# Padding the products on 64 rows and on 64 or 32 columns to full 128 by 128

## The chip, the cores and the metric

The kernel runs on one core of a Trainium2 chip. The metric is the device time of one execution in microseconds (us), lower is better. Matrix products run on TensorE (PE in the profile, its weight loads apart as PEld), elementwise work on VectorE (DVE), ScalarE (ACT) and GpSimd (POOL). Transfers are issued by SyncE (SP).

## What is computed

The reference is one transformer-like layer on x of shape (4, 512, 128): a gated convolution block, then a mixture of 160 small experts, each behind a layer norm with a scale and a shift.

```python
h = _layernorm(x) * (1 + ca) + sa
# attention-free block: D = 128, DI = 256
h = _rmsnorm(h, norm_w); h = _linear(h, in_w, in_b)
gate, val = sigmoid(h[..., :DI]), h[..., DI:]
a = dwconv4(val) @ A @ Bm                 # then ha_w
b = linear(silu(dwconv9(val)), pw_w)      # then hb_w
x = x + ga * (h_in + linear(gate * fuse(concat(a, b)), out_w))
h = _layernorm(x) * (1 + cb) + sb
# experts: 160 of them, top 8, inner size 64
probs = sigmoid(h @ router_w.T + expert_bias)
combine = top-8 weights of probs, normalised, times 2.5
routed = sum_e (silu(h @ w_gate[e].T) * combine[:, e]) @ w_down[e]
shared = silu(h @ w_gate_shared.T) @ w_down_shared.T
x = x + gb * (routed + shared)
```

## The kernel before

The batch is worked in four chunks c = 0 to 3 of 512 tokens. Most products carry a value as the sum of two half-precision parts (a high and a low one). The helper `split` (lines 954 to 956) therefore issues three half-precision matmuls for one product, each on 512 columns of tokens: one at L954, one at L955, one at L956. Every such product in the kernel has these three lines, so they are told apart by the tiles they read.

The experts are taken in pairs, and two pairs make a duo. A chunk has 40 duos, the kernel 160. `duo(J)` issues on PE two up-projections of duo J (`bank<-x_h,w`, each 3 matmuls) and two down-projections of duo J-4 (`bank<-g_all,w`, each 3 matmuls). Between them ACT applies silu (L648), DVE multiplies by the routing weights (L931), ACT rounds to half precision (L667), and DVE takes the remainder (L927). The routing weights come from DRAM, where `c_out` has put them, and are loaded for every duo (L409).

`walk` is the order of the work, written out by hand, and every engine follows it. Chunk 0's block, and most of chunk 1's, run in a prologue before the first duo. After that, the steps of chunk c+1 (table `REST`) and c+2 (tables `FRONT` and `TAPS`) are put between the duos of chunk c, so the router of chunk 1 runs between the duos of chunk 0, and so on. The steps that matter here, on PE:

- `conv0`, `conv1`: nine taps of three matmuls each, then one matmul for the borders and the bias, on 64 rows: `rsym` (64 rows) against the constant `isym` (L1042). Twice a chunk, 8 in all.
- `logit`: for each of 4 groups of 128 tokens, one matmul on 64 rows for the expert bias (`ones2` against `rrtr`, L1109), and one `split` product of 160 columns (`bank<-rsg_h,x_h`). 16 groups in all. ACT's `prob` (L630) follows, then the top-8 search on DVE (L901, L905, L911, L921).
- `shup`: the shared expert's up-projection. Its stationary operand is the last 64 columns of `rsg_h` and `rsg_l`, so 64 rows of the result bank are written. One `split` product a chunk, followed by ACT's silu `ss` (L636).
- `cT`: the routing weights (160 columns) turned by transposes. Four turn columns 0 to 127 (L1122), four turn the other 32 columns (L1125). ACT copies the result to `cT0` and `cT1` (L641, L643), and SP writes it to DRAM (L426, L428).
- the shared expert's down-projection, `sdw` against `ss32`, both on 64 rows and in single precision (L1150). One a chunk, at the first down-projection of the chunk. It waits until ACT has emptied the accumulator of the chunk before (L676). A single-precision matmul shows as two records.

The first rows of `rsym` and `rrtr` (0 to 31) are written by ACT and rows 32 to 63 by DVE in `setup(5)` and `setup(8)`, once. `rsg` and `sdf` are loaded once, in the prologue, ahead of the expert weights, and turned into `rsg_h`, `rsg_l` (L549, L765) and `sdw` (L551).

Of the kernel before, what the change touches and what calls it, by code (L numbers as in the profile page):

```python
# [209 lines left out]
def build(nc, x, vecs, mats, wmod_d, outT_d, consts, rows, frow_d, symT, rsgT, sdT, idf_c, w_d, out):  # L210
# [3 lines left out]
    with ExitStack() as ctx:  # L214
# [16 lines left out]
        outT = sb("outT", [P, ML, D])  # L231
        rsg = sb("rsg", [P, E + INTER])
        sdf = sb("sdf", [INTER, P])
        sdw = sb("sdw", [INTER, P])
        win_h, win_l = sb("win_h", [P, DI], F16), sb("win_l", [P, DI], F16)
# [5 lines left out]
        zs = sb("zs", [P, 2, L], F16)  # L241
        rsg_h, rsg_l = sb("rsg_h", [P, E + INTER], F16), sb("rsg_l", [P, E + INTER], F16)
        row4 = sb("row4", [B, MODC])
# [3 lines left out]
        ebias, outb = brow[0:64, 0:E], brow[:, E:E + D]  # L247
        rsym = sb("rsym", [64, DI], F16)
        rrtr = sb("rrtr", [64, E], F16)
        gob = sb("gob", [P, D])  # L250
# [15 lines left out]
        x_l = [sb(f"x_l{i}", [P, L], F16) for i in range(2)]  # L266
        ss32 = sb("ss32", [INTER, L])
        pr, key, cw = (sb(n, [P, NT, E]) for n in ("pr", "key", "cw"))
# [7 lines left out]
        yT = sb("yT", [P, L])  # L276
        cT0, cT1 = sb("cT0", [P, L]), sb("cT1", [E - P, L])
        dum = sb("dum", [P, 1])
# [30 lines left out]
        def k(name, rows=P):  # L309
# [3 lines left out]
        s = {n: sem(n) for n in (  # L313
            "ld_vec ld_wmod ld_mat ld_outT ld_cst ld_rows ld_frow ld_sym ld_rsg ld_sd ld_idf ld_mod row_out w_hi w_lo "
            "x_in0 x_in1 x_in2 x_in3 pool_zero pads zs_zero zs_one eps_set one_set scb_set mod_ps mod_half mod_set row_ps row_half row_set "
# [46 lines left out]
        def _(sp):  # L362
# [49 lines left out]
            def att(c, n):  # L412
                if n == "zmv":
                    if c:
                        sp.wait_ge(s["y_ps"], 2 * c)
                    else:
                        sp.wait_ge(s["zs_zero"], 1)
                        sp.wait_ge(s["zs_one"], 1)
                    sp.wait_ge(s["zh_set"], c + 1)
                    sp.wait_ge(s["zl_set"], c + 1)  # L420
                    for q in range(DC):
                        w = slice(32 * q, 32 * q + DS)
                        sp.dma_start(zs[w], zp[w, :, q:q + L]).then_inc(s["z_mv"], 16)
                elif n == "c_out":
                    sp.wait_ge(s["cT_set"], 2 * c + 1)
                    sp.dma_start(cd[c, 0:P, :], cT0[:]).then_inc(s["c_out"], 16)  # L426
                    sp.wait_ge(s["cT_set"], 2 * c + 2)
                    sp.dma_start(cd[c, P:E, :], cT1[:]).then_inc(s["c_out"], 16)  # L428

# [15 lines left out]
        def _(pool):  # L445
            g = nc.gpsimd
            g.memset(hnT[:, :, 0:PADL], 0.0).then_inc(s["pads"], 1)
            g.memset(hnT[:, :, PADL + L:], 0.0).then_inc(s["pads"], 1)
            g.memset(mhalf[:], -0.5).then_inc(s["eps_set"], 1)
            g.memset(eps5[:], 1e-5).then_inc(s["eps_set"], 1)  # L450
# [45 lines left out]
        def _(act):  # L496
# [13 lines left out]
            def setup(n):  # L510
# [18 lines left out]
                elif n == 5:  # L529
                    taps_hi(2)  # L530
                    act.wait_ge(s["sc_ps"], 1)
                    a(rsym[0:32], A3[0:32, 0:DI], ACT.Copy, scale=ES)
                    a(tmp_h[32:64, 0], A3[32:64, 0:DI], ACT.Copy, scale=ES).then_inc(s["sc_hi"], 1)
# [26 lines left out]
            def att(c, n):  # L560
# [71 lines left out]
                elif n == "ss":  # L632
                    act.wait_ge(s["sh_ps"], c + 1)
                    if c:
                        act.wait_ge(s["sd_ps"], c)
                    a(ss32[:], TB[0:INTER, :], ACT.Silu, scale=1.0 / ES).then_inc(s["ss_set"], 1)  # L636
                elif n == "cT_sb":
                    if c:
                        act.wait_ge(s["c_out"], 32 * c)
                    act.wait_ge(s["cT_ps"], 2 * c + 1)  # L640
                    a(cT0[:], A4[:], ACT.Copy).then_inc(s["cT_set"], 1)  # L641
                    act.wait_ge(s["cT_ps"], 2 * c + 2)
                    a(cT1[:], A3[0:E - P, :], ACT.Copy).then_inc(s["cT_set"], 1)  # L643

# [302 lines left out]
        def _(pe):  # L947
# [67 lines left out]
            def att(c, n):  # L1015
# [15 lines left out]
                elif n[0:4] == "conv":  # L1031
# [7 lines left out]
                    if i1 == KS:  # L1039
                        if c + q == 0:  # L1040
                            pe.wait_ge(s["sc_lo"], 1)
                        mm(bk[:], rsym[:, q * P:(q + 1) * P], k("isym", 64), start=False, stop=True).then_inc(s["conv_ps"], 1)  # L1042
                elif n == "z":
# [53 lines left out]
                elif n == "logit":  # L1097
# [6 lines left out]
                    for t in range(NT):  # L1104
# [3 lines left out]
                        dst = (A4, A3)[t // 2][:, t % 2 * E:(t % 2 + 1) * E]  # L1108
                        mm(dst, k("ones2", 64), rrtr[:], start=True, stop=False)  # L1109
                        b = c % 2  # L1110
# [3 lines left out]
                elif n == "shup":  # L1114
                    pe.wait_ge(s["xl_set"], c + 1)
                    b = c % 2
                    split(TB[0:INTER, :], (rsg_h[:, E:], rsg_l[:, E:]), (x_h[b][:], x_l[b][:])).then_inc(s["sh_ps"], 1)
                elif n == "cT":
# [5 lines left out]
                    for t in range(NT):  # L1124
                        last = turn(A3[0:E - P, t * P:(t + 1) * P], cw[:, t, P:E], idf[:])  # L1125
                    last.then_inc(s["cT_ps"], 1)
# [102 lines left out]
```

## Time and profile before

| | |
|---|---|
| median of 3 runs | 573.82 us (571.63 to 575.61) |
| the profiled execution's own time | 573.52 us |
| its span, first to last instruction | 571.7 us |
| mean granted TensorE clock | 0.987 |
| busy in the span: PE, DVE, ACT, POOL | 544.1, 474.0, 414.4, 29.6 us |

A matmul's duration in a record includes the time that it takes to run through the array, while the next one has already begun. The duration of a record is therefore not what it costs. The cost is read from the distance between the starts of one matmul and the next. In a timeline, the first column is the start in us, the second the duration in us, and `x4` means that four like instructions were merged into one row. A note in brackets at the end is the time that the engine sat idle before it, with what ended the wait.

### The profile page before, as it was taken

To read this page: it belongs to the slowest core of one execution; us is meant where nothing else is said; L and a number is where in the kernel's file an instruction comes from. 1 tells how busy PE (TensorE), PEld (TensorE's weight loads), DVE (VectorE), ACT (ScalarE), POOL (GpSimd) and SP (SyncE) were. 2 spreads that over 40 slices of the span, in tenths; PEclk is the share of its full clock that TensorE was granted. 3 is DMA by queue.
4 is the path that set the end of the run, shared out by engine and by line. 5 is a ranking of instruction groups with operands and counts; after the bars stand their busy time and mean duration, and the time that the engine had idled before them with its cause. 6 is when DMAs were issued, how large, how long until landed. Compare 5 with 4: busy or idle time off the path is not lost.

```text
span 571.7 us, 7315 instructions
## 1 busy us (share of the span) xinstructions
PE 544.1 (95%) x2528; PEld 251.4 (44%) x2528; DVE 474.0 (83%) x600; ACT 414.4 (72%) x668; POOL 29.6 (5%) x52
## 2 busy tenths in 40 slices
PE   5697889999999999999999999999989999999996
PEld 3334424543444444454444444454434444444442
DVE  5676479999959988799859688789959988999995
ACT  5446488789777776779666686568876877777773
POOL 5011000050000000011000000002000000000000
PEclk9797999999999999999999999999999999999999
DMA  7976075445534655455544455455635666566650
GB/s 265 346 258 263 10 248 180 150 150 179 185 110 148 204 187 176 146 169 199 158 138 148 170 185 174 148 181 188 213 119 180 231 201 203 198 207 205 200 186 18
DMA packets 33244, 103.26 MB, mean 181 GB/s; under 512 B 3700, under 2 KB 9013, under 8 KB 32952
## 3 DMA queue, kind: packets, MB, share of 16 engines
q1 hardware_dynamic: 33208, 102.81, 53.3%
q8 instruction: 20, 0.33, 0.2%
q14 instruction: 16, 0.13, 0.1%
HBM read 99.90 MB, written 2.37 MB: 179 GB/s over the span
## 4 chain that ended last, share of the span: by engine, by line
PE 78%; DVE 9%; ACT 5%; issue 4%; DMA 2%; POOL 1%; SPq 0%; ACTq 0%; DVEq 0%
PE bank L954 24%; PE bank L955 24%; PE bank L956 24%; DVE g_all L927 2%; DVE s_all L931 2%; PE bank L1075 2%; ACT g_all L667 1%; DMA c_all<-combine 1%; PE bank L1085 1%; DMA g_all<-wmod_dram 1%; ACT s_all L648 1%; DVE w L791 1%; PE bank L1150 1%; ACT hnT L594 1%; PE bank L1109 0%
## 5 line engine op out<-in xcount | busy, mean ns | idle before, releaser
L648 ACT ACTIVATE s_all<-bank 128x512 f32<-128x512 f32 x320 | 189.4, 593 | 109.6 <-PE bank L956 105.9
L927 DVE TENSOR_TENSOR g_all<-s_all,g_all 128x1024 f16<-128x1024 f32 x160 | 195.3, 1221 | 55.6 <-ACT g_all L667 55.1
L931 DVE TENSOR_TENSOR s_all<-s_all,c_all 128x1024 f32<-128x1024 f32 x160 | 194.8, 1218 | 3.9 <-DMA c_all<-combine 3.4
L667 ACT ACTIVATE g_all<-s_all 128x1024 f16<-128x1024 f32 x160 | 168.0, 1050 | 3.4 <-DVE s_all L931 3.3
L954 PE MATMUL bank<-x_h,w 128*128 128x512 f16 x320 | 121.4, 380 | 4.1 <-ACT s_all L648 4.0
L954 PE MATMUL bank<-g_all,w 128*128 128x512 f16 x320 | 121.4, 379 | 2.7 <-DVE g_all L927 2.7
L955 PE MATMUL bank<-g_all,w 128*128 128x512 f16 x320 | 121.3, 379 | 0.0
L956 PE MATMUL bank<-g_all,w 128*128 128x512 f16 x320 | 121.3, 379 | 0.0
L956 PE MATMUL bank<-x_l,w 128*128 128x512 f16 x320 | 121.3, 379 | 0.0
L955 PE MATMUL bank<-x_h,w 128*128 128x512 f16 x320 | 121.3, 379 | 0.0
L954 PEld LDWEIGHTS bank<-x_h,w 128*128 128x128 f16 x320 | 31.3, 98 | 46.9 <-ACT s_all L648 10.0
L954 PEld LDWEIGHTS bank<-g_all,w 128*128 128x128 f16 x320 | 31.3, 98 | 44.7 <-DVE g_all L927 7.5
L956 PEld LDWEIGHTS bank<-g_all,w 128*128 128x128 f16 x320 | 31.3, 98 | 37.8
L956 PEld LDWEIGHTS bank<-x_l,w 128*128 128x128 f16 x320 | 31.3, 98 | 37.8
L955 PEld LDWEIGHTS bank<-g_all,w 128*128 128x128 f16 x320 | 31.3, 98 | 36.6
L955 PEld LDWEIGHTS bank<-x_h,w 128*128 128x128 f16 x320 | 31.3, 98 | 35.4 <-issue 2.0
L954 PE MATMUL bank<-hnT,wc_h 128*128 128x512 f16 x72 | 28.6, 397 | 1.2 <-ACT hnT L594 1.2
L955 PE MATMUL bank<-hnT,wc_l 128*128 128x512 f16 x72 | 28.5, 395 | 0.0
L956 PE MATMUL bank<-hnT,wc_h 128*128 128x512 f16 x72 | 28.3, 393 | 0.0
L791 DVE SCALAR_TENSOR_TENSOR w<-w 128x1024 f16<-128x1024 f32 x20 | 24.2, 1216 | 4.0 <-ACT w L558 3.9
L558 ACT ACTIVATE w<-w 128x1024 f16<-128x1024 f32 x20 | 20.8, 1052 | 5.0 <-DVE w L791 5.0
L484 POOL TENSOR_TENSOR mse<-ms,eps 128x4 f32<-128x4 f32 x4 | 6.0, 1496 | 193.2 <-ACT hr_h L575 193.2
(212 smaller groups left out, 367.6 us busy)
## 6 DMA issues: line engine op xcount, KB each, us to landing
c_all<-combine SPq DMA_DIRECT2D x160, 512.0 KB, 3.9
w<-w_dram SPq DMA_DIRECT2D x20, 512.0 KB, 8.9
s_all<-mats_dram SPq DMA_DIRECT2D x1, 1152.0 KB, 7.6
attw<-symT_dram SPq DMA_DIRECT2D x1, 1152.0 KB, 10.3
res<-x_dram SPq DMA_DIRECT2D x4, 256.0 KB, 9.0
combine<-cT SPq DMA_DIRECT2D x4, 256.0 KB, 3.1
out_dram<-res SPq DMA_DIRECT2D x4, 256.0 KB, 2.4
mod<-rows_mod SPq DMA_DIRECT2D x1, 960.0 KB, 6.5
```

Of the source, the lines that this page charges most:

```text
L484: g.tensor_tensor(mse[:], ms[:], eps6[:], ALU.add).then_inc(s["mse_set"], 1)
L558: a(high(i), staged(i), ACT.Copy, scale=ES).then_inc(s["w_hi"], 1)
L594: a(hnT[:, :, PADL:PADL + L], TBh.rearrange("p (a l) -> p a l", a=2), ACT.Copy)\
L648: a(sr[J % SRING][:, q * L:(q + 1) * L], U[q][:], ACT.Silu, scale=1.0 / ES).then_inc(s["s_done"], 1)
L667: a(gh[n % GRING], sr[n % SRING], ACT.Copy).then_inc(s["hi_set"], 1)
L791: e.scalar_tensor_tensor(out=low(i), in0=staged(i), scalar=ES, in1=high(i), op0=ALU.mult, op1=ALU.subtract).then_inc(s["w_lo"], 1)
L927: e.tensor_tensor(gl[n % GRING], sr[n % SRING], gh[n % GRING], ALU.subtract).then_inc(s["lo_set"], 1)
L931: e.tensor_tensor(sr[J % SRING], sr[J % SRING], cr[J % CRING], ALU.mult).then_inc(s["gm"], 1)
L954: mm(dst, lh, rh, start=start, stop=False)
L955: mm(dst, ll, rh, start=False, stop=False)
L956: return mm(dst, lh, rl, start=False, stop=stop)
L1075: last = mm((A1, A2)[q][:], wb[:, i, q * P:(q + 1) * P], s32[:, i, :], start=False, stop=(i == ML - 1))
```

## The change

The operands that had 64 rows get 128, the added ones zero. The operands that had 64 or 32 columns get 128.

- `rsym` and `rrtr` get 128 rows, and POOL sets them to zero at the start (two memsets). ACT waits for these (`rows_zero`) before it writes the first part of `rsym`. L1042 and L1109 read all 128 rows of the constants, whose added rows are zero already.
- `rsg` gets 64 zero columns behind its 224, and with it `rsg_h` and `rsg_l`. `shup` takes 128 columns and writes the whole bank, `ss32` has 128 rows.
- `sdf` and `sdw` get 64 zero rows, so the product at L1150 is on 128 rows.
- The second half of `cT` turns columns 32 to 159 in place of 128 to 159. The 32 wanted rows then are rows 96 to 127 of the bank, and the copy and the DRAM write take them from there.

```diff
-        rsg = sb("rsg", [P, E + INTER])
-        sdf = sb("sdf", [INTER, P])
-        sdw = sb("sdw", [INTER, P])
+        rsg = sb("rsg", [P, E + P])
+        sdf = sb("sdf", [P, P])
+        sdw = sb("sdw", [P, P])
...
-        rsg_h, rsg_l = sb("rsg_h", [P, E + INTER], F16), sb("rsg_l", [P, E + INTER], F16)
+        rsg_h, rsg_l = sb("rsg_h", [P, E + P], F16), sb("rsg_l", [P, E + P], F16)
...
-        rsym = sb("rsym", [64, DI], F16)
-        rrtr = sb("rrtr", [64, E], F16)
+        rsym = sb("rsym", [P, DI], F16)
+        rrtr = sb("rrtr", [P, E], F16)
...
-        ss32 = sb("ss32", [INTER, L])
+        ss32 = sb("ss32", [P, L])
...
-        cT0, cT1 = sb("cT0", [P, L]), sb("cT1", [E - P, L])
+        cT0, cT1 = sb("cT0", [P, L]), sb("cT1", [P, L])
...
-                    sp.dma_start(cd[c, P:E, :], cT1[:]).then_inc(s["c_out"], 16)
+                    sp.dma_start(cd[c, P:E, :], cT1[2 * P - E:]).then_inc(s["c_out"], 16)
...
+            g.memset(rsym[:], 0.0).then_inc(s["rows_zero"], 1)
+            g.memset(rrtr[:], 0.0).then_inc(s["rows_zero"], 1)
...
+                    act.wait_ge(s["rows_zero"], 2)
...
-                    a(ss32[:], TB[0:INTER, :], ACT.Silu, scale=1.0 / ES).then_inc(s["ss_set"], 1)
+                    a(ss32[:], TB[:], ACT.Silu, scale=1.0 / ES).then_inc(s["ss_set"], 1)
...
-                    a(cT1[:], A3[0:E - P, :], ACT.Copy).then_inc(s["cT_set"], 1)
+                    a(cT1[2 * P - E:], A3[2 * P - E:, :], ACT.Copy).then_inc(s["cT_set"], 1)
...
-                        mm(bk[:], rsym[:, q * P:(q + 1) * P], k("isym", 64), start=False, stop=True).then_inc(s["conv_ps"], 1)
+                        mm(bk[:], rsym[:, q * P:(q + 1) * P], k("isym"), start=False, stop=True).then_inc(s["conv_ps"], 1)
...
-                        mm(dst, k("ones2", 64), rrtr[:], start=True, stop=False)
+                        mm(dst, k("ones2"), rrtr[:], start=True, stop=False)
...
-                    split(TB[0:INTER, :], (rsg_h[:, E:], rsg_l[:, E:]), (x_h[b][:], x_l[b][:])).then_inc(s["sh_ps"], 1)
+                    split(TB[:], (rsg_h[:, E:], rsg_l[:, E:]), (x_h[b][:], x_l[b][:])).then_inc(s["sh_ps"], 1)
...
-                        last = turn(A3[0:E - P, t * P:(t + 1) * P], cw[:, t, P:E], idf[:])
+                        last = turn(A3[:, t * P:(t + 1) * P], cw[:, t, E - P:], idf[:])
```

The host adds the zero columns to `rsg` and the zero rows to `sdT`. All else is as before.

## Rows read from the trace of the kernel before

**Rows 1.** The page's part 1: busy time, share and instructions of each engine.

```profile
PE 544.1 (95%) x2528; PEld 251.4 (44%) x2528; DVE 474.0 (83%) x600; ACT 414.4 (72%) x668; POOL 29.6 (5%) x52
```

**Rows 2.** Windows: stretch, length, busy PE, PEld, DVE, ACT, POOL, clock, DMA.

```profile
20.00:40.00 20.00, 20.00 (x80) 9.17 (x78) 12.69 (x46) 6.02 (x12) 2.48 (x2) 0.89 0.71 270
139.00:414.00 275.00, 274.64 (x1297) 127.57 (x1296) 234.89 (x270) 203.68 (x318) 7.64 (x6) 1.00 0.51 169
```

**Rows 3.** Timeline of PE: start, duration, line, tiles, shapes; the end of a convolution.

```profile
166.51 0.38 PE L954 MATMUL bank<-hnT,wc_h 128*128 128x512 f16 x1
...
166.94 0.38 PE L956 MATMUL bank<-hnT,wc_h 128*128 128x512 f16 x1
167.26 0.39 PE L1042 MATMUL bank<-cst,rsym 64*128 64x512 f16 x1
167.57 0.39 PE L954 MATMUL bank<-hnT,wc_h 128*128 128x512 f16 x1
167.80 0.38 PE L955 MATMUL bank<-hnT,wc_l 128*128 128x512 f16 x1
```

**Rows 4.** Timeline of PE: router and shared up-projection of chunk 1.

```profile
157.00 0.38 PE L956 MATMUL bank<-g_all,w 128*128 128x512 f16 x1
...
157.49 0.24 PE L954 MATMUL bank<-rsg_h,x_h 128*128 128x160 f16 x1
157.56 0.23 PE L955 MATMUL bank<-rsg_h,x_l 128*128 128x160 f16 x1
157.63 0.23 PE L956 MATMUL bank<-rsg_l,x_h 128*128 128x160 f16 x1
...
159.09 0.23 PE L956 MATMUL bank<-rsg_l,x_h 128*128 128x160 f16 x1
159.26 0.40 PE L954 MATMUL bank<-x_h,rsg_h 128*64 128x512 f16 x1
...
160.02 0.39 PE L954 MATMUL bank<-x_h,w 128*128 128x512 f16 x1
```

**Rows 5.** Timeline of PE: the transposes of the routing weights, chunk 1.

```profile
187.02 0.60 PE L1122 MATMUL bank<-idf,cw 128*128 128x128 f32 x4
187.45 0.60 PE L1125 MATMUL bank<-idf,cw 128*32 128x128 f32 x4
187.89 0.38 PE L954 MATMUL bank<-hnT,wc_h 128*128 128x512 f16 x1
```

**Rows 6.** Groups by line and form: weight loads of these transposes; busy us, mean ns.

```profile
L1122 PEld LDWEIGHTS bank<-idf,cw 128*128 128x128 f32 x16 | 1.8, 141 | 3.2 <-DVE cw L921 2.9
...
L1125 PEld LDWEIGHTS bank<-idf,cw 128*32 128x32 f32 x16 | 1.6, 97 | 0.1
```

**Rows 7.** Timeline of PE: the shared down-projection of chunk 1.

```profile
215.21 1.12 PE L1150 MATMUL bank<-ss,sdw 64*128 64x512 f32 x2 [0.18 <-ACT yT L676]
216.26 0.39 PE L954 MATMUL bank<-g_all,w 128*128 128x512 f16 x1
```

**Rows 8.** Timeline of PE: single-precision products on 128 rows, in the prologue's wake.

```profile
95.19 1.88 PE L1075 MATMUL bank<-attw,wb 128*128 128x512 f32 x4
96.91 0.38 PE L954 MATMUL bank<-x_h,w 128*128 128x512 f16 x1
```

**Rows 9.** Chain of waits in order of time, prologue: start, us, what.

```profile
22.24 0.43 PE bank L954
...
65.12 0.45 ACT pr L630
```

**Rows 10.** Timeline of DVE in the prologue.

```profile
45.64 0.39 DVE L765 SCALAR_TENSOR_TENSOR rsg_l<-rsg,rsg_h 128x224 f16<-128x224 f32 x1
```

**Rows 11.** Timeline of ACT behind the router of chunk 3.

```profile
418.60 0.60 ACT L648 ACTIVATE s_all<-bank 128x512 f32<-128x512 f32 x1 [3.38 <-PE bank L956]
```

**Rows 12.** Timeline of ACT behind the router of chunk 1.

```profile
168.74 0.59 ACT L648 ACTIVATE s_all<-bank 128x512 f32<-128x512 f32 x1
```

**Rows 13.** Timeline of PE, the up-projection that waits for the silu of rows 12.

```profile
169.53 0.38 PE L954 MATMUL bank<-x_h,w 128*128 128x512 f16 x1
```

More of the change, by code:

```diff
@@ L313, in build @@
         s = {n: sem(n) for n in (
-            "ld_vec ld_wmod ld_mat ld_outT ld_cst ld_rows ld_frow ld_sym ld_rsg ld_sd ld_idf ld_mod row_out w_hi w_lo "
+            "rows_zero ld_vec ld_wmod ld_mat ld_outT ld_cst ld_rows ld_frow ld_sym ld_rsg ld_sd ld_idf ld_mod row_out w_hi w_lo "
             "x_in0 x_in1 x_in2 x_in3 pool_zero pads zs_zero zs_one eps_set one_set scb_set mod_ps mod_half mod_set row_ps row_half row_set "
@@ L1196 @@
         w["in_w"].T, w["in_w"][DI:], w["ha_w"].T, w["hb_w"].T, w["pw_w"], w["fuse_w"].T)], 1)
-    rsg = np.concatenate([f["router_w"].T, f["w_gate_shared"].T], 1)
+    spare = np.zeros((P, P - INTER), np.float32)
+    rsg = np.concatenate([f["router_w"].T, f["w_gate_shared"].T, spare], 1)
     two = np.zeros((P, P), np.float32)
@@ L1217 @@
               "consts": consts.astype(np.float16), "rows": rows, "frow": w["fuse_b"][None],
-              "symT": w["sym_k"].reshape(DI, KS).T.reshape(1, KS * DI), "rsgT": rsg, "sdT": f["w_down_shared"].T,
+              "symT": w["sym_k"].reshape(DI, KS).T.reshape(1, KS * DI), "rsgT": rsg, "sdT": np.concatenate([f["w_down_shared"].T, spare.T]),
               "idf": np.eye(P, dtype=np.float32), "w": wall}
```

## Prediction

> **What bounds the kernel now.** I began with the busy times. PE is busy for 95% of the span [rows 1], DVE for 83%, so PE is the first suspect. The table of stretches says where this holds: from 139 to 414 us PE is busy 274.64 of 275 us, at the full granted clock of 1.00, that is 2.4 GHz, while DVE is busy 234.89 [rows 2]. "Busy" hides short stalls, since a record lasts 0.38 us and the next starts sooner, so I then went through the PE timeline by starts. In the normal stream three matmuls of 512 columns lie within 0.43 us from first start to last, 0.216 a step (166.51 to 166.94 is two steps) [rows 3]. Wherever a start comes later than that, PE has lost time that no busy figure shows. In this stretch nearly all such losses sit beside matmuls on 64 rows or with 64 columns.
>
> The prologue, a stretch before 139 us and one behind the router of chunk 3 are bounded by chains through ACT, DVE and DMA. There I followed the chain of waits in order of time, to see which changed products lie on it.
>
> **The border product of a convolution (L1042, 8 of them).** From the last full matmul at 166.94 to the second one behind it at 167.80 there are 0.86 us for three steps [rows 3]. Three normal steps are 0.65. The 64-row product starts 0.32 after its predecessor, its successor 0.31 after it, and one more step is 0.01 late: 0.21 us lost around a matmul that itself streams the same 512 columns. With 128 rows I take all of it to go. Four of the eight (chunks 2 and 3) lie between duos of the PE-bound stretch: 4 x 0.21 = 0.84 us. One of chunk 1's lies on the prologue's chain (below). Both of chunk 0's and the second of chunk 1's lie where PE afterwards waits for DVE, ACT or a DMA. That wait covers them, and I count nothing (0.6 us if the cover were gone).
>
> The Trainium skill, page TensorEngine Tiling (Array Packing), section Tiling Modes, Key Properties, says that a change of tiling mode drains TensorE. That would make 64 rows, and 64 columns, modes of their own, entered and left each time, which is what the starts show; it gives no duration, and the sum needs none from it.
>
> **Router and shared up-projection (L1109, `rsg_h`).** A full product of 160 columns takes 0.07 us from start to start (157.56 to 157.63) [rows 4]. By columns alone it would be 0.216 x 160/512 = 0.068, so I take 0.069. From 157.00 to the first up-projection at 160.02 there are 3.02 us. In full shape this is 0.216 + 16 x 0.069 + 3 x 0.216 = 1.97. With the 0.01 behind it, 1.06 us are saved a chunk. Part of this is the 64-column product: its first matmul starts 0.17 after its predecessor, not 0.07, and from its start to the next duo there are 0.76 us where 3 x 0.216 = 0.65 would do; its share is 0.22, that of the 64 rows 0.84.
>
> Chunks 1 to 3 save this on the path: 3 x 1.06 = 3.18 us. For chunk 3 the time behind it is bounded by ACT and DVE, not PE. But ACT was idle for 3.38 us waiting just for this up-projection [rows 11], so it starts 1.06 earlier, and the chain behind it shifts whole.
>
> **Prologue.** The chain runs through PE, including one border product, up to the end of the router of chunk 0, then to `prob` at 65.12 [rows 9], the top-8 search, the transposes and the DRAM round trip of the routing weights. The saving is 0.21 + 0.84 = 1.05 us; `shup` is off this chain.
>
> **The shared down-projection (L1150, 4).** Its two records and the step to the next take 1.05 us [rows 7]. Single-precision products on 128 rows take (96.91 - 95.19) / 4 = 0.43 each [rows 8], so 0.86 for two: 0.20 saved with the 0.01 behind. The wait in front of it, for ACT's L676, stays. Chunk 0's is covered by a wait for DVE. 3 x 0.20 = 0.60 us.
>
> **The transposes (L1125, 16).** Wide ones take 187.45 - 187.02 = 0.43 for four, narrow ones 0.44 [rows 5]. Nothing is lost at the 32 columns, so nothing is won. The load of 128 columns lasts 141 ns against 97 [rows 6], but lies beside the products, since the wide ones already keep the pace. Without that cover: 16 x 44 ns = 0.7 us.
>
> Here a rule speaks against the change. The Trainium skill, TensorE: Matmul & The Clock Gate, section LDWEIGHTS, puts a load at its column count over 1.2 GHz, so four times as long for 128 as for 32. By it the 16 loads would grow by 80 ns each, an estimate of 1.3 us if exposed; the trace grows them by 44 ns and hides them.
>
> **Additions.** The two POOL memsets come before POOL's first wait, for the statistics of chunk 0, which come later than they end. ACT comes to its new wait only behind the first convolution weights, and so long after them that nothing queues behind it. `rsg_l` works on 288 columns in place of 224: 0.39 us [rows 10] becomes at most 0.39 x 288/224 = 0.50, 0.11 more on DVE, ahead of the gating of chunk 0. This is beside the chain, which runs through chunk 1's normalisation then; 0.1 us if not. The loads of `rsg` and `sdf` grow by 64 KB together, ahead of the weights on SP's queue; at the 270 GB/s of that time [rows 2] this is 0.24 us on weights that are used later. The silu, copies and DRAM write keep their columns; partitions are free. For these together: 0 to 0.4, taken 0.
>
> **Sum.** 1.05 + 3.18 + 0.84 + 0.60 = 5.67 us. The profiled execution took 573.52, so 567.85; the median of the runs is 0.30 higher, so 568.15, rounded to **568.2 us**, 1.0% below.
>
> **Rivals.**
>
> A. *Part of the gain turns into waits.* Where PE speeds up, the slack to ACT and DVE must hold. The tightest place I found behind a router is the up-projection at 169.53, whose silu ended at 168.74 + 0.59 = 169.33 [rows 12, 13]: 0.20 us, while the border product at 167.26 gives 0.21. That costs 0.01. Larger losses would need the prologue's or chunk 3's chain to hold on something that doesn't move, say the DMA of the routing weights. Without these two, 1.05 + 1.06 less: 5.67 - 2.11 = 3.56 saved, **570.3 us**. Against it: the 3.38 us of idle ACT. Chance 0.08.
>
> B. *Only the rows cost, not the columns.* Then the three `shup` on the path keep 0.22 each: 5.0 saved, **568.8 us**. Or the wide weight loads show, 0.7: the same figure. Against it: starts are late on entering and on leaving the 64 columns [rows 4]. But the transposes show that 32 columns need not cost [rows 5]. Chance 0.07.
>
> C. *The change doesn't do what it says:* the late starts come from something else about these products (a constant as an operand, the start of an accumulation). **573.8 us**. Against it: three kinds with nothing else in common show the same 0.1 on each side. Chance 0.04.
>
> D. *Slower:* the granted clock. At half clock (1.2 GHz) a matmul of 512 columns takes 0.43 us, as at 22.24 [rows 9], where the stretch's clock is 0.89 [rows 2]. The router of chunk 0 gets shorter, while the waits around it (the search, then the DRAM round trip) stay, so PE is idle for a larger share of 60 to 83 us. If the clock fell there and stayed low into the first duos, each matmul would cost 0.21 more. It decides from 5.67 / 0.21 = 27 matmuls on, some 12 us at half clock. For over 1% slower it takes twice that, **579.6 us**. Against it: PE already waits there, and with 0.89 in one early stretch [rows 2] the mean over the whole span is still 0.987, which leaves little at half clock later. Chance 0.03.
>
> The forecast itself has 0.78.
>
> **How the numbers follow.** About 1% is what a measurement of this kernel can tell from no change. That bound lies at 568.08, within 0.1 us of the forecast, so the forecast's chance is split between faster and the same. Three runs of before spread over 4 us, which puts 1.5 us on either side of a median. More mechanisms take from the sum than add to it. Faster by over 1%: 0.45, from the forecast (0.43) and B (0.02). Within 1%: 0.52, the rest of the forecast (0.35), the rest of B (0.05), A and C. Slower: 0.03, which is D. The range goes up to A with some spread on it, 571.3, and down by the spread and for a chain that gives more than its sum, 565.8. C, D and the tails are left out.
>
> **What would show it.** Right: starts 0.216 apart through each border product; router and `shup` of chunks 1 to 3 in 1.97 us; two records of L1150 in 0.86; the same 0.11 for each transpose; the idle ACT at 418 down from 3.38 to 2.3. Wrong: starts still late by 0.1 at these products (C, or B where only `shup` is late), new idle time in front of L954 with ACT or DVE as the releaser (A), a clock under 1.00 between 60 and 100 us (D).

## The result and the profile after

| | before | after |
|---|---|---|
| median of 4 runs of each, side by side | 574.14 us (571.63 to 575.61) | 566.68 us (565.39 to 569.14) |
| the profiled execution's own time | 573.52 us | 567.25 us |
| its span | 571.7 us | 565.2 us |
| mean granted TensorE clock | 0.987 | 0.986 |

The ratio is 0.9897, with the interval [0.9873, 0.9921]. (The quotient of the two medians is 0.9870; four runs of each leave a difference of that size, and I use the ratio with its interval.) Two later series of the same kernel gave 0.9929 [0.9913, 0.9945] and 0.9908 [0.9892, 0.9924]; in the first of them one execution took 2006 us and is left out. The mean of the three is 0.991, against 568.15 / 573.82 = 0.990 forecast. Whether the gain is over or under 1%, which the forecast left open, these intervals leave open too. Lines stand three lower than before: L954 to L956 are now L957 to L959, L1042 is L1045, L1150 is L1153.

Part 1 of the page of the kernel after, which answers to [rows 1]:

```profile
PE 537.8 (95%) x2528; PEld 253.4 (45%) x2528; DVE 474.6 (84%) x600; ACT 415.4 (73%) x668; POOL 29.4 (5%) x54
```

PE has as many instructions as before and 6.3 us less busy time, and the span is 6.5 us shorter.

The PE timeline of the kernel after, the end of a convolution, which answers to [rows 3]:

```profile
163.59 0.38 PE L959 MATMUL bank<-hnT,wc_h 128*128 128x512 f16 x1
163.81 0.38 PE L1045 MATMUL bank<-cst,rsym 128*128 128x512 f16 x1
164.02 0.38 PE L957 MATMUL bank<-hnT,wc_h 128*128 128x512 f16 x1
```

The starts are 0.22 and 0.21 apart. The 0.1 on each side is gone. Next, the router and the shared up-projection of chunk 1, which answer to [rows 4]:

```profile
154.71 0.38 PE L959 MATMUL bank<-g_all,w 128*128 128x512 f16 x1
154.93 0.23 PE L1112 MATMUL bank<-rrtr,cst 128*128 128x160 f16 x1
...
155.97 0.23 PE L959 MATMUL bank<-rsg_l,x_h 128*128 128x160 f16 x1
156.03 0.38 PE L957 MATMUL bank<-x_h,rsg_h 128*128 128x512 f16 x1
...
156.68 0.38 PE L957 MATMUL bank<-x_h,w 128*128 128x512 f16 x1
```

From 154.71 to 156.68 there are 1.97 us, as forecast, in place of 3.02.

I then set the starts of the same matmul in both traces against each other, all through the program. The lead of the kernel after, in us:

| up to | lead | what gave it |
|---|---|---|
| 52.4 us, second convolution of chunk 0's block | 0.02 | |
| end of the router of chunk 0 | 2.55 | 1.45 from a shorter stretch at half clock, 1.08 from the change |
| first down-projection of a duo, 80.59 | 2.28 | 0.27 lost again |
| router and `shup` of chunk 1 | 3.34 | 1.06 |
| border products of chunk 2 | 3.68 | -0.06 in front of an up-projection, 0.40 |
| behind `sdw` of chunk 1 | 3.78 | 0.10 |
| router and `shup` of chunk 2 | 4.85 | 1.07 |
| border products of chunk 3, `sdw` of chunk 2 | 5.37 | 0.41, 0.11 |
| router and `shup` of chunk 3, its `sdw` | 6.52 | 1.06, 0.09 |

The 1.45 us are no work of the change: in the profile of before, a stretch at half clock (starts 0.43 us apart) lasts from 48.5 to 55.3 us, in that of after only from 47.8 to 51.2. The windows show it, in the column in front of the last two; before, then after:

```profile
40.00:60.00 20.00, 16.06 (x67) 8.27 (x65) 11.64 (x28) 13.11 (x33) 2.42 (x4) 0.83 0.63 252
```

```profile
40.00:60.00 20.00, 16.05 (x74) 9.22 (x75) 11.39 (x28) 13.32 (x34) 2.42 (x4) 0.91 0.61 243
```

The length of this stretch doesn't go with the change. In the runs below it is 6.8 us again in `x64cols` and `late`, which have all of the change, and 3.4 us in `grouped`, which pads nothing. So the change itself gave 6.52 - 1.45 = 5.07 us, where 5.67 were forecast.

### The profile page after: what moved, and what is told of

Read it like the earlier page. It is cut to its first block, busy times and chain, and to the rows that moved or that the text cites. A ratio compares the mean times of both kernels' runs of the same rounds, so it can differ in the third digit from the quotient of the medians.

```text
span 565.2 us, 7318 instructions
## 1 busy us (share of the span) xinstructions
PE 537.8 (95%) x2528; PEld 253.4 (45%) x2528; DVE 474.6 (84%) x600; ACT 415.4 (73%) x668; POOL 29.4 (5%) x54
## 4 chain that ended last, share of the span: by engine, by line
PE 78%; DVE 9%; ACT 6%; issue 4%; DMA 2%; POOL 0%; SPq 0%; ACTq 0%; DVEq 0%
PE bank L957 24%; PE bank L959 24%; PE bank L958 24%; DVE g_all L930 2%; DMA attw<-symT_dram 2%; PE bank L1078 2%; DVE s_all L934 2%; ACT g_all L670 1%; ACT s_all L651 1%; PE bank L1088 1%; PE bank L1153 1%; DVE w L794 1%; ACT hnT L597 1%; ACT w L561 0%; ACT yT L679 0%
## 5 line engine op out<-in xcount | busy, mean ns | idle before, releaser
L930 DVE TENSOR_TENSOR g_all<-s_all,g_all 128x1024 f16<-128x1024 f32 x160 | 195.4, 1221 | 52.4 <-ACT g_all L670 51.9
L957 PE MATMUL bank<-x_h,w 128*128 128x512 f16 x320 | 121.4, 379 | 3.9 <-ACT s_all L651 3.7
L957 PE MATMUL bank<-g_all,w 128*128 128x512 f16 x320 | 121.3, 379 | 2.1 <-DVE g_all L930 2.1
L959 PE MATMUL bank<-g_all,w 128*128 128x512 f16 x320 | 121.3, 379 | 0.0
L959 PE MATMUL bank<-x_l,w 128*128 128x512 f16 x320 | 121.3, 379 | 0.0
L957 PEld LDWEIGHTS bank<-x_h,w 128*128 128x128 f16 x320 | 31.3, 98 | 46.0 <-ACT s_all L651 10.0
L957 PEld LDWEIGHTS bank<-g_all,w 128*128 128x128 f16 x320 | 31.3, 98 | 42.0 <-DVE g_all L930 5.0
L959 PEld LDWEIGHTS bank<-g_all,w 128*128 128x128 f16 x320 | 31.3, 98 | 37.8
L959 PEld LDWEIGHTS bank<-x_l,w 128*128 128x128 f16 x320 | 31.3, 98 | 37.8
L957 PE MATMUL bank<-hnT,wc_h 128*128 128x512 f16 x72 | 28.5, 396 | 1.2 <-ACT hnT L597 1.2
L959 PE MATMUL bank<-hnT,wc_h 128*128 128x512 f16 x72 | 28.8, 400 | 0.0
```

The lines of the kernel that those rows point to most:

```text
L930: e.tensor_tensor(gl[n % GRING], sr[n % SRING], gh[n % GRING], ALU.subtract).then_inc(s["lo_set"], 1)
L957: mm(dst, lh, rh, start=start, stop=False)
L959: return mm(dst, lh, rl, start=False, stop=stop)
```

## What the theory and its rivals are now

The theory: TensorE is late by about 0.1 us on entering a product on 64 rows or with 64 columns, and by as much again on leaving it. The rivals: only rows cost (B); something else about these products costs (C). Three things were open after the result: where the limit lies, whether the cost goes by product or by change of shape, and why the prologue gave back 0.27 us (rival D, at a small scale).

## Experiment 1: the disputed cost by itself

A product is added to each of the 160 duos of the kernel after, in the middle of an up-projection. It multiplies zeros, so nothing in the result changes. `x128` is the control with a full product, `x64rows` has 64 rows, `x64cols` 64 columns.

```diff
+        zt = sb("zt", [P, P], F16)          # zeros
...
-                        split(U[q][:], pair(J, q, 0), (x_h[b][:], x_l[b][:])).then_inc(s["up_ps"], 1)
+                        (wh, wl), xh = pair(J, q, 0), x_h[b]
+                        mm(U[q][:], wh, xh[:], start=True, stop=False)
+                        mm(U[q][:], wl, xh[:], start=False, stop=False)
+                        if q == 0:
+                            mm(U[q][:], zt[:], xh[:], start=False, stop=False)              # x128
+                            mm(U[q][:], zt[0:64], xh[0:64], start=False, stop=False)        # x64rows
+                            mm(U[q][0:64], zt[:, 0:64], xh[:], start=False, stop=False)     # x64cols
+                        mm(U[q][:], wh, x_l[b][:], start=False, stop=True).then_inc(s["up_ps"], 1)
```

Only one of the three marked lines stands in each kernel.

> The changed kernel with one more half-precision matmul in each of the 160 duos: a tile of zeros as the stationary operand, on 128 rows and 128 columns, 512 columns of tokens, between the second and the third matmul of the duo's first up-projection. It adds zero to the result. It is the control for the two runs beside it. All theories: 160 x 0.216 = 34.6 us, less a little where DVE and ACT bound the time. With 567 us for the changed kernel, about 600 us. Starts 0.216 apart around the added matmul.

> As the control, but the added matmul is on 64 rows (zeros and the first 64 rows of the tokens), between matmuls on 128 rows. Theory (a change of the number of rows costs 0.10 us on entering and 0.10 on leaving): 0.21 us more for each of the 160, so 33 us above the control, about 632 us, with the added matmul 0.31 behind its predecessor and its successor 0.31 behind it. Rival C (the late starts came from other properties of the three products, such as a constant as operand or the start of an accumulation; none of these is here): the same as the control, 600 us.

> As the control, but the added matmul has 64 stationary columns and writes 64 rows of the bank. Theory (a change of columns costs like a change of rows): about 0.2 us each, 632 us. Rival B (only rows cost, the columns in shup were late for another reason): 600 us, as the control.

| | median, us | ratio to before |
|---|---|---|
| x128 | 597.06 | 1.0441 [1.0403, 1.0479] |
| x64rows | 627.69 | 1.0970 [1.0938, 1.1003] |
| x64cols | 631.08 | 1.1011 [1.0966, 1.1056] |

Against the control, 64 rows cost 30.6 us more, 0.19 for each of 160, and 64 columns 34.0 us, 0.21 each. The PE timelines of one place show it; first the control, then 64 rows, then 64 columns. The added product is at L1152.

```profile
301.37 0.38 PE L1150 MATMUL bank<-x_h,w 128*128 128x512 f16 x1
301.59 0.38 PE L1152 MATMUL bank<-x_h,zt 128*128 128x512 f16 x1
301.81 0.38 PE L1153 MATMUL bank<-x_l,w 128*128 128x512 f16 x1
```

```profile
301.54 0.38 PE L1150 MATMUL bank<-x_h,w 128*128 128x512 f16 x1
301.85 0.39 PE L1152 MATMUL bank<-x_h,zt 64*128 64x512 f16 x1
302.17 0.39 PE L1153 MATMUL bank<-x_l,w 128*128 128x512 f16 x1
```

```profile
300.78 0.38 PE L1150 MATMUL bank<-x_h,w 128*128 128x512 f16 x1
301.09 0.40 PE L1152 MATMUL bank<-x_h,zt 128*64 128x512 f16 x1
301.42 0.39 PE L1153 MATMUL bank<-x_l,w 128*128 128x512 f16 x1
```

In the control all steps are 0.22. With 64 rows or columns the step to the product is 0.31, the step from it 0.32 or 0.33, and the one behind it 0.22 or 0.23. Operand, accumulation and place are the same in all three, so C is out for good, and so is B: columns cost as much as rows. The control adds some 30 us over the kernel after, not 160 x 0.216 = 34.6. Before 139 us PE is not always the bound: in the window from 102 to 139 us it was busy 35.08 of 37 us before and 36.98 in the control, so part of the added work went into idle time.

## Experiment 2: where the limit lies

`shapes` is the kernel after with other counts of rows and columns at the places that the change touches. The places with 32 rows leave out the low part of the bias.

```diff
+                        r = {(1, 0): 33, (2, 0): 32, (2, 1): 96, (3, 0): 64, (3, 1): 65}.get((c, q), P)
+                        mm(bk[:], rsym[0:r, q * P:(q + 1) * P], k("isym", r), start=False, stop=True).then_inc(s["conv_ps"], 1)
...
+                        r = {1: (32, 64, 96, 33), 2: (48, 65, 80, 112), 3: (64, 32, 64, 128)}.get(c, (P,) * NT)[t]
+                        mm(dst, k("ones2", r), rrtr[0:r], start=True, stop=False)
...
+                    n_ = {1: 96, 2: 80, 3: 65}.get(c, P)
+                    split(TB[0:n_], (rsg_h[:, E:E + n_], rsg_l[:, E:E + n_]), (x_h[b][:], x_l[b][:])).then_inc(s["sh_ps"], 1)
```

> The changed kernel with other numbers of rows at single places, to read the starts there. Border products: 33 rows (chunk 1, first), 32 and 96 rows (chunk 2), 64 and 65 rows (chunk 3). Bias products of the router: 32, 64, 96, 33 rows in chunk 1, 48, 65, 80, 112 rows in chunk 2, 64, 32, 64, 128 in chunk 3. Shared up-projection on 96, 80 and 65 columns in chunks 1 to 3. The places with 32 rows leave out the low part of the border or bias. Theory (the array is set to a tile of 32, 64 or 128 rows, and what lies between is rounded up): 32, 33, 48 and 64 rows show 0.10 on each side, 65, 80, 96 and 112 rows show nothing, and so for the columns, where 96, 80 and 65 show nothing. Rival (anything short of 128 costs): all show 0.10 on each side. The time moves by 1 to 2 us against the changed kernel.

Its one execution took 569.14 us, which says nothing by itself. Its PE timeline does. Router of chunk 1, with 32 rows, then 96, then 33:

```profile
154.81 0.38 PE L959 MATMUL bank<-g_all,w 128*128 128x512 f16 x1
155.12 0.24 PE L1114 MATMUL bank<-rrtr,cst 32*128 32x160 f16 x1
155.29 0.24 PE L957 MATMUL bank<-rsg_h,x_h 128*128 128x160 f16 x1
...
155.92 0.23 PE L959 MATMUL bank<-rsg_l,x_h 128*128 128x160 f16 x1
155.99 0.23 PE L1114 MATMUL bank<-rrtr,cst 96*128 96x160 f16 x1
156.07 0.23 PE L957 MATMUL bank<-rsg_h,x_h 128*128 128x160 f16 x1
...
156.21 0.23 PE L959 MATMUL bank<-rsg_l,x_h 128*128 128x160 f16 x1
156.37 0.24 PE L1114 MATMUL bank<-rrtr,cst 33*128 33x160 f16 x1
```

The steps to and from 32 rows are 0.31 and 0.17, those to and from 96 rows 0.07 and 0.08, and that to 33 rows is 0.16. The other places agree. 32, 33, 48 and 64 rows are late by 0.1 on each side; 65, 80, 96 and 112 rows not at all. For columns, 65 (the up-projection at chunk 3) is enough too:

```profile
412.45 0.23 PE L959 MATMUL bank<-rsg_l,x_h 128*128 128x160 f16 x1
412.52 0.38 PE L957 MATMUL bank<-x_h,rsg_h 128*65 128x512 f16 x1
...
413.17 0.38 PE L957 MATMUL bank<-x_h,w 128*128 128x512 f16 x1
```

The Trainium skill, TensorEngine Tiling (Array Packing), section Tiling Modes, lists 32, 64 and 128 rows and columns as the configurations, and says that changing between them drains the engine. By that rule 65 rows, which no tile of 64 holds, would run as 128. The trace agrees: a padding of one row beyond 64 is enough, and all 128 aren't needed.

## Experiment 3: by product or by change of shape

`grouped` is the kernel before, with only the order in the router changed: the four 64-row bias products first, then the four `split` products. With this goes that the wait for `x2_set` comes ahead of the first of them, and that of the two groups of a bank only the first has `start=True`.

```diff
+                    dst = [(A4, A3)[t // 2][:, t % 2 * E:(t % 2 + 1) * E] for t in range(NT)]
+                    pe.wait_ge(s["x2_set"], c + 1)
                     for t in range(NT):
-                        if t == 2:
-                            pe.wait_ge(s["x2_set"], c + 1)
+                        mm(dst[t], k("ones2", 64), rrtr[:], start=(t % 2 == 0), stop=False)
+                    for t in range(NT):
...
-                        dst = (A4, A3)[t // 2][:, t % 2 * E:(t % 2 + 1) * E]
-                        mm(dst, k("ones2", 64), rrtr[:], start=True, stop=False)
...
-                        last = split(dst, (x_h[b][:, w], x_l[b][:, w]), (rsg_h[:, 0:E], rsg_l[:, 0:E]), start=False)
+                        last = split(dst[t], (x_h[b][:, w], x_l[b][:, w]), (rsg_h[:, 0:E], rsg_l[:, 0:E]), start=False, stop=bool(t % 2))
```

> The kernel before, nothing padded, but the four bias products on 64 rows of a chunk's router stand together, ahead of the four split products, so that the number of rows changes once in and once out in place of four times. Theory (the cost sits at a change of rows, not at a product on 64 rows): two of the four starts stay late, 0.21 us, and 3 x 0.21 = 0.63 us go in each chunk, 2.5 us in all, ratio 0.9956. The four 64-row products start 0.07 apart. Rival (each product on 64 rows costs, wherever it stands): they start 0.16 or more apart, and the time stays at 574.

It took 569.62 us, a ratio of 0.9967 [0.9948, 0.9986]. Its PE timeline, chunk 1:

```profile
158.06 0.38 PE L956 MATMUL bank<-g_all,w 128*128 128x512 f16 x1
158.38 0.45 PE L1107 MATMUL bank<-rrtr,cst 64*128 64x160 f16 x4
158.76 0.24 PE L954 MATMUL bank<-rsg_h,x_h 128*128 128x160 f16 x1
```

The step into the group is 0.32. From the first of the four to the matmul behind them there are 0.38: three steps of about 0.07 and a last one of 0.16. So four 64-row products in a row pay once, and it is the change of shape that costs, not the product. Of 0.84 a router this order saves some 0.63, or 2.5 us for four, 0.44%, forecast as 0.9956. The ratio agrees, but its interval alone would also allow 0.14%; the steps carry this.

## Experiment 4: one part alone, and the kernels once more

`rows_only` is the kernel before with the padding of rows in `rsym`, `rrtr` and the constants alone. `shup`, `sdw` and the transposes keep their shapes. The two memsets and the wait for `rows_zero` are in it too. `again` and `again2` are the kernel after and `before_again` the kernel before, unchanged.

```diff
-        rsym = sb("rsym", [64, DI], F16)
-        rrtr = sb("rrtr", [64, E], F16)
+        rsym = sb("rsym", [P, DI], F16)
+        rrtr = sb("rrtr", [P, E], F16)
...
-                        mm(bk[:], rsym[:, q * P:(q + 1) * P], k("isym", 64), start=False, stop=True).then_inc(s["conv_ps"], 1)
+                        mm(bk[:], rsym[:, q * P:(q + 1) * P], k("isym"), start=False, stop=True).then_inc(s["conv_ps"], 1)
...
-                        mm(dst, k("ones2", 64), rrtr[:], start=True, stop=False)
+                        mm(dst, k("ones2"), rrtr[:], start=True, stop=False)
```

> The kernel before with only the rows of the half-precision products padded (the border product and the router's bias, L1042 and L1109); the shared expert's two products and the transposes stay narrow. Theory: of the sum, the prologue's 1.05, three routers at 0.84 and four border products at 0.21 remain: 4.4 us saved, ratio 0.992. The shared up-projection still starts 0.17 behind its predecessor and the next duo 0.31 behind it.

> The changed kernel once more, for its ratio and for where the half clock (1.2 GHz) lies in another execution. Theory (the profiled execution owed about 1.4 us of its 6.5 to a half-clock stretch that ended sooner, which is luck): over more executions the ratio comes nearer to 1 - 5.2/574 = 0.991. Rival (the change itself brings the clock up sooner): the half-clock stretch at 48 to 55 us is short here too, and the ratio is 0.988 or less.

> The kernel before, profiled once more. Theory (where the half clock ends is luck): its half-clock stretch near 50 us ends at another time than 55.3 us, or has another length than 6.8 us. Rival (the kernel sets it): the same place and length as before, within 0.3 us.

> The changed kernel once more on another occasion. Theory (the sum holds but for 0.3 us at the shared down-projection and 0.3 us in the DMA round trip of the prologue, and the clock adds or takes some 1.5 us from one execution to the next): ratio 0.990 to 0.992. Rival (the shorter router costs clock on average): 0.993 or more, and mean granted clocks lower than in the runs of the kernel before beside it.

`rows_only` took 566.69 us, ratio 0.9912 [0.9878, 0.9947]; `before_again` 572.64 us in its one execution; `again` and `again2` gave the ratios told above.

On where the half clock lies, `again` says nothing, since its profile is of the execution of 2006 us. In `again2` the stretch near 50 us is 3.4 us long, from 48.0 to 51.4, nearly as in the kernel after. In `before_again` there is none near 50 us, as the theory of luck allowed. The rival that expected a ratio of 0.993 or more with lower mean clocks is right about the clocks: 0.987 on average in `again` and `again2`, against 0.990 in the runs of the kernel before beside them. The ratios are 0.9929 and 0.9908, one at its border and one not. I come back to this below.

By the steps, `rows_only` should lack 3 x (0.22 + 0.10) = 0.96 us, or 0.17%, of the change. The intervals are wider than that, so the times don't separate the two. The PE timeline does; here the shared up-projection of chunk 1 in `rows_only`:

```profile
155.36 0.23 PE L959 MATMUL bank<-rsg_l,x_h 128*128 128x160 f16 x1
155.52 0.40 PE L957 MATMUL bank<-x_h,rsg_h 128*64 128x512 f16 x1
...
156.29 0.39 PE L957 MATMUL bank<-x_h,w 128*128 128x512 f16 x1
```

It starts 0.16 after its predecessor, not 0.06 as in the kernel after, and 0.77 us pass to the next duo, not 0.65.

## What the prologue gave back

The prologue was forecast to give 1.05 us. It gave 1.08 by the end of the router, but 0.27 were lost before the first down-projection. The windows of 20 us from 60 to 80 show the place (stretch, length, busy PE, PEld, DVE, ACT, POOL, clock, DMA share, GB/s): before, then a second profile of it, then `rows_only`, then the kernel after.

```profile
60.00:80.00 20.00, 16.67 (x85) 7.04 (x84) 9.32 (x22) 12.90 (x20) 0.00 (x0) 1.00 0.32 107
```

```profile
60.00:80.00 20.00, 16.36 (x84) 6.92 (x83) 10.17 (x23) 13.34 (x21) 0.00 (x0) 1.00 0.38 123
```

```profile
60.00:80.00 20.00, 16.01 (x83) 6.88 (x80) 12.42 (x25) 14.15 (x23) 0.00 (x0) 1.00 0.42 154
```

```profile
60.00:80.00 20.00, 16.69 (x81) 7.57 (x80) 12.58 (x25) 13.99 (x22) 0.00 (x0) 0.91 0.41 155
```

The clock falls to half for a time in the kernel after, and not in the others. The chain of waits of the kernel after (start, us, what) names who feels it:

```profile
71.31 0.43 PE bank L959
71.74 0.27 PE bank L1045
72.08 0.60 ACT attw L604
...
79.90 0.86 PE bank L1153 x2
```

These are taps of the second convolution of chunk 1, at 0.43 a step from 68.3 to 71.7 us. Before, the chain ran here through the DRAM round trip of the routing weights instead:

```profile
71.38 1.79 DMA combine<-cT
...
73.88 5.35 DMA c_all<-combine
```

The time from the first transpose of `cT` to the first down-projection of a duo, in the profiles that have the same order of work between the two:

| kernel | half clock between 60 and 90 us | PE idle before `cT`, us | cT to down-projection, us |
|---|---|---|---|
| before | none | 1.70 | 82.88 - 69.59 = 13.29 |
| before_again | none | 1.70 | 82.02 - 68.84 = 13.18 |
| rows_only | none | 1.69 | 79.99 - 66.93 = 13.06 |
| after | 68.3 to 71.7 | 1.92 | 80.59 - 67.05 = 13.54 |
| again2 | 68.5 to 71.9 | 1.92 | 81.21 - 67.67 = 13.54 |
| shapes | 66.9 to 70.3 | 1.92 | 80.68 - 66.71 = 13.97 |
| grouped | 78.7 to 85.5 | 1.83 | 82.43 - 67.55 = 14.88 |

With the stretch, the kernel after takes 0.25 us more than before and 0.48 more than `rows_only`. In `shapes` it falls on the transposes themselves and takes 0.68 more than before. In `grouped`, which pads nothing, it falls on the first duos and takes 1.6 more.

A stretch near 70 us stands in all seven profiles that have the full change and none of the fillers of experiment 5 (after, again2, shapes, late and the three of experiment 1), in neither of before and not in `rows_only`. That is the place and the mechanism of rival D, at a small part of the loss that would have made the kernel slower. Of the shapes that `rows_only` keeps, the shared down-projection can't bring the stretch on, since it comes at 79.7 us. The shared up-projection can: padded, it is over 0.22 us sooner, and PE then waits 1.92 us in front of the transposes in place of 1.70. That fits D, but no run changes it alone, and `grouped` shows that such a stretch can come without the change. With one profile for most kernels this is an association, not a proof.

The mean clocks of the other executions point the same way. They average 0.987 in each of `again`, `again2` and `late`, against 0.990 in the runs of the kernel before beside them and 0.9915 in `rows_only`. One stretch of 3.4 us at half clock takes 3.4 x 0.5 / 566 = 0.003 from the mean, an estimate. But it isn't in every execution: two of the first four had 0.986 and 0.987, the other two 0.994, and these two were the fastest, 565.39 and 566.12 us.

## Experiment 5: no half clock, and no wait at the shared down-projection

`warm` is the kernel after with 34 useless matmuls in places where PE would be idle in the prologue. They write to a bank that nobody reads before it is started anew. In the order of the cuts they stand before the first transposes of chunk 0, behind these of chunks 0 and 1, before the output projection of chunk 0, and before the transposes of its routing weights.

```diff
+            def spin(k_):
+
+                for _ in range(k_):
+                    mm(U1[:], k("id"), k("isym"))
...
+                    if c == 0:
+                        pe.wait_ge(s["mod_half"], 2)
+                        spin(11)
...
+                    if c < 2:
+                        spin(4)
...
+                        if c == 0:
+                            spin(7)
...
+                    if c == 0:
+                        spin(8)
```

`late` is the kernel after with both up-projections of a chunk's first duo ahead of its first down-projection, so that the wait for ACT's L679 is over when PE comes to it. `best` has both.

```diff
-                for q in range(2):
+                def up(q):
...
+                def down(q):
...
+                if d == 0:
+                    up(0), up(1), down(0), down(1)
+                else:
+                    up(0), down(0), up(1), down(1)
```

> The changed kernel with idle PE time in the prologue filled by matmuls whose result is not used (identity against the constant of the border product, into a free bank): 11 before the first transposes of chunk 0, 4 behind these of chunks 0 and 1, 7 before chunk 0's output product, 8 before chunk 0's routing weights are turned. Theory (the half clock comes from PE's waits in the prologue, and what it costs is what spreads the times): the half-clock stretches near 17 to 24 us and 48 to 51 us shrink or go, their matmuls start 0.216 and not 0.43 apart, the mean granted clock rises above 0.995, and the time falls by 2 to 5 us against the changed kernel, with less spread. Rival (the half clock comes at these times whatever PE does): the same time or up to 2 us more, for the added matmuls that run over into work.

> The changed kernel with another order at the first duo of a chunk: both up-projections ahead of the shared down-projection and the two down-projections, so that the wait of PE for ACT's emptying of the accumulator is covered. Theory: the start of L1153's product behind its predecessor falls from 0.56 to 0.22 us and its first record's step from 0.53 to 0.43, 0.44 us at three places: 1.3 us. Rival (ACT and DVE wait in its stead): the next down-projections start late and nothing is won.

> Both additions together: the filled prologue and the later wait. If both theories hold, 3 to 6 us below the changed kernel.

| | median, us | ratio to before |
|---|---|---|
| again2 | 567.09 (566.80 to 567.71) | 0.9908 [0.9892, 0.9924] |
| warm | 563.49 (562.87 to 566.15) | 0.9853 [0.9833, 0.9874] |
| late | 567.19 (565.34 to 568.72) | 0.9901 [0.9884, 0.9918] |
| best | 563.09 (561.66 to 565.94) | 0.9843 [0.9820, 0.9866] |

`warm` is 3.6 us faster than the kernel after. The smaller spread that was expected did not come: its executions lie 3.3 us apart, all at mean clocks of 0.997 to 1.000, so the spread has another source besides. Its windows have the full clock throughout the prologue:

```profile
0.00:20.00 20.00, 12.68 (x63) 7.36 (x64) 13.17 (x39) 12.57 (x35) 10.26 (x38) 1.00 0.92 301
20.00:40.00 20.00, 18.70 (x84) 9.12 (x83) 14.28 (x47) 8.51 (x16) 2.48 (x2) 1.00 0.83 311
40.00:60.00 20.00, 18.93 (x107) 10.18 (x106) 11.32 (x31) 12.28 (x32) 2.41 (x4) 1.00 0.53 208
60.00:80.00 20.00, 17.59 (x81) 7.40 (x79) 14.14 (x24) 15.87 (x23) 0.00 (x0) 1.00 0.57 187
```

Its last router product of chunk 0 starts at 58.92, against 62.30 in the kernel after; from there the time from `cT` to the down-projection is 76.47 - 63.67 = 12.80, against 13.54. Together that is 4.1 us, the difference of the spans (561.1 and 565.2). The Trainium skill, TensorE: Matmul & The Clock Gate, section HAM oscillation, says that a kernel with waits between its bursts of matmuls swings between the two clocks, and advises to restructure it. The traces agree that idle stretches and half clock go together: in the first 20 us PE is busy 9.86 us at a mean clock of 0.93 in the kernel after, and 12.68 us at 1.00 in `warm`; in front of the transposes of `cT` it is idle for 1.92 us and for 0.20. Here useless matmuls in the idle time were enough.

`late` did to PE what it was meant to. Its PE timeline at chunk 1, and that of the kernel after:

```profile
214.47 0.38 PE L959 MATMUL bank<-x_l,w 128*128 128x512 f16 x1
214.69 1.02 PE L1155 MATMUL bank<-ss,sdw 128*128 128x512 f32 x2
215.55 0.38 PE L957 MATMUL bank<-g_all,w 128*128 128x512 f16 x1
```

```profile
211.52 1.12 PE L1153 MATMUL bank<-ss,sdw 128*128 128x512 f32 x2 [0.18 <-ACT yT L679]
212.48 0.38 PE L957 MATMUL bank<-g_all,w 128*128 128x512 f16 x1
```

Behind a wait the two records and the step to the next take 0.96; without the wait 0.86. The start behind the predecessor falls from 0.56 to 0.22. That is 0.44 us at each of three places, as expected. From the second down-projection of the duo that has `sdw` to that of the next chunk it takes 131.43, 128.97 and 118.69 us in place of 131.89, 129.41 and 119.14: 1.35 us in all.

Yet the time is the same, 567.19 against 567.09. The rival holds at chunk 0, which has no such wait: the down-projections come later there, and from the first transpose of `cT` to the second of them it takes 84.76 - 69.31 = 15.45 us in place of 81.89 - 67.05 = 14.84. `best` loses the like against `warm`, 14.64 against 14.11. So 0.7 to 0.8 us remain, too little to be seen in these medians (`best` is 0.4 below `warm`). The profile of `late` can't show it in its span either, since its stretch near 50 us is 6.8 us long. Had the new order been kept to chunks 1 to 3, the loss should have gone; no run has that.

## Why the prediction was right, and where it missed

**Right: the border products.** Forecast 0.21 each; the four on PE's path gave 0.40 + 0.41. Chunk 1's in the prologue gave 0.20.

**Right: router and `shup`.** 1.06 us each time, three times, and 1.97 us for the stretch. Chunk 3's shifted as forecast: the idle time of ACT [rows 11] fell from 3.38 to 2.31 us in the ACT timeline of the kernel after.

```profile
412.16 0.60 ACT L651 ACTIVATE s_all<-bank 128x512 f32<-128x512 f32 x1 [2.31 <-PE bank L959]
```

**Right: the transposes.** The four that turned 32 columns [rows 5] still take 0.44 us, with weight loads of 142 ns beside them in place of 97 [rows 6]. The PE timeline of the kernel after, then its groups by form:

```profile
183.97 0.60 PE L1128 MATMUL bank<-idf,cw 128*128 128x128 f32 x4
184.41 0.38 PE L957 MATMUL bank<-hnT,wc_h 128*128 128x512 f16 x1
```

```profile
L1128 PEld LDWEIGHTS bank<-idf,cw 128*128 128x128 f32 x16 | 1.9, 142 | 0.0
```

**Missed: the shared down-projection.** Forecast 0.20 each, measured 0.10. The step that failed took 0.43 a record from [rows 8], where such products follow one another without a wait. This one comes behind a wait, and its first step is 0.53 us in the kernel before as in the kernel after; only the second fell, from 0.52 to 0.43. `late` shows that the wait is what makes the difference, and so does chunk 0's product in the kernel after, which has no wait: 0.43 + 0.43. 0.3 us less than forecast. One thing stays open: on 64 rows both records of this product are late by 0.1, though nothing changes its shape between them.

**Missed: the prologue.** 1.05 were forecast, 1.08 gained and 0.27 lost again. Rival D named the place and the mechanism, and I gave it only the price at which it would turn the sign. The step that failed took every saving of the chain for whole, although the chain changes its way there: with the change it ran through PE, at half clock. What I held against D was wrong too. A mean clock of 0.987 over 571.7 us is about 15 us at half clock, and the window that I named holds 4.4 of them; the trace of before had the 6.8 us from 48.5 us on as well, on the prologue's chain.

**Missed, small: rival A.** 0.06 us were lost at an up-projection that waits for ACT's silu [rows 12, 13], where 0.01 was forecast.

The misses, 0.30 + 0.24 + 0.06, make the 0.60 us between 5.67 and 5.07. By these steps alone the kernel after should take 573.5 - 5.1 = 568.4 us.

**Luck.** The profiled execution took 567.25 us, near the 567.85 forecast for it, because 1.45 us from the shorter half-clock stretch stood against 0.60 us of misses. That the first series came out lower than 568.4 is within the spread of the executions, of which the half clock in the prologue is a part: its two fastest are those with a mean clock of 0.994, and `before_again`, with one such stretch before 60 us in place of two, took 0.9 us less than the profiled execution of before.

**Right: the additions.** They cost nothing on the path: `rsg_l` takes 0.46 us on DVE in place of 0.39 [rows 10], and POOL's memsets end before 1.3 us.

## What to carry to other kernels

Read PE's starts, not its busy time: a matmul on few rows or columns can cost 0.2 us more than it streams, and an engine at 95% busy doesn't show it. Where narrow products stand alone between full ones, pad them past 64, or put them one behind the other so that the shape changes once. Then look at PE's granted clock slice by slice: filling idle time in the prologue with useless matmuls gave 3.6 us, where the whole change gave 4.9 in the same series. A gain of this size is seen in the starts of a trace long before it is seen in the time: padding the rows alone (`rows_only`) can't be told from the full change by its runs.

## What the runs showed of the hardware that was not expected

- The limit lies between 64 and 65, for rows (65, 80, 96 and 112 cost nothing) and for columns (65, 80, 96): padding to 128 isn't needed.
- Half-precision products with 64 columns are late on each side by 0.1 us, yet single-precision transposes of 32 columns are not (0.44 for four, narrow or wide). No run tells whether precision, the transpose or the 32 columns makes the difference.
- The first record of a single-precision product behind a wait takes 0.53 us, on 64 rows as on 128; on 128 rows without a wait it takes 0.43.
- Half clock in the prologue comes and goes from one execution to the next: stretches of 3 to 10 us, near 17, 50 and 70 us, of which the kernel before had two in one profile and one in the other. One that was 3.4 us shorter gave 1.45 us.
